# Window attention of a four-layer image model: scores as four 32-row products instead of one masked 128-row product

## The chip, the cores and the metric

The kernel is one program on one core of a Trainium2 chip. The metric is device time in microseconds (us) of one execution. Before the change three runs gave 7491.1, 7505.19 and 7510.78 us; the median is 7505.19 us. Most executions of one kernel agree within 0.3%.

## The reference: what is computed

The input is an fp32 image batch `x` of shape (4, 64, 128, 128). Eight stages follow each other (four pairs of a mixing layer and a feed-forward layer), each added to its input. The change touches only the first, a shifted-window attention:

```python
x = x + _L0_conv_ref(_ln_c(x), qkv_w, proj_w, proj_b, bias_table)
# DIM = 64, WS = 8 (windows of 8 x 8 = 64 pixels), NH = 4 heads,
# SHIFT = 4, HD = 16 channels of a head, SCALE = HD ** -0.5 = 0.25
#   q, k, v = the normalised image, rolled by 4, cut into windows, times qkv_w
#   scores  = SCALE * q @ k.T + relative position bias + shift mask
#   out     = softmax(scores) @ v, then proj_w and proj_b, rolled back
```

For each image, window and head the scores are a 64 x 64 matrix with a contraction over 16 channels. There are 256 windows in an image. The softmax is exact, with the row maximum taken off.

## The kernel before

Each stage is a function that writes one instruction stream for each engine (TensorE, VectorE, ScalarE, GpSimd and SyncE) by hand. Engines wait for each other only through semaphores, and each engine keeps the order in which its stream was written. `stage_window_attention` is the first stage; the others begin after it.

**Tiling.** Two images are worked on at once: 128 partitions are 2 images x 64 channels. `over_strips` runs twice (`bp`), each time over 16 strips of 8 image rows (16 windows side by side). The first strip and the last three are written out, the twelve between are a loop of four strips in a body. A strip has four steps, j = 0 to 3, of STEP = 4 windows for both images (T = 256 pixels). So the stage has 2 x 16 x 4 = 128 steps. `steps` gives each step s its neighbours: `after` is s + 1, `back1` is s - 1, `back2` is s - 2.

**One step, before the change.**

- TensorE, `qkv`: q and k of four windows into `pQK` (two products of 256 columns, line 567), v into `pV` (four of 128 columns, line 572).
- ScalarE, `save_qk`: `pQK` goes to SBUF in six copies. Two copies (line 455) write `qs`, one for each image g: the mask `gmask` keeps the 64 channels of image g, zeroes the others and holds SCALE. Four copies (line 458) write `ks`, one for each head: the mask `hmask` keeps the 16 channels of head k in both images and zeroes the rest.
- TensorE, `scores` (line 579): per window one product with 128 rows of contraction. Stationary are 128 columns (2 images x 64 queries), moving are 256 columns (4 heads x 64 keys). The output is `pS[128, STEP, NH, 64]`, two PSUM banks.
- VectorE, `softmax_shift`: bias added while `pS` is read (line 393; in step j = 3 the last window by itself at line 391), maximum (397), subtraction (399). ScalarE, `exponential` (464). VectorE, `softmax_sum`: sum (404), reciprocal (406). GpSimd, `normalise` (309).
- TensorE `turn_probs` (588), ScalarE `save_probs` (469), TensorE `values` (598: 16 products of 64 columns, each with 128 rows and 32 output partitions), ScalarE `save_values` (474), TensorE `project` (604), ScalarE `save_proj` (481).

**What goes between the steps.** The layer norm of the next strip is spread over the steps of the strip: `mean` (611), VectorE `center` (412), ScalarE `square` (487), `variance` (620), ScalarE `log` (492) and `root` (498), each with a change of activation table, and `write_h` on VectorE and GpSimd (225). At j = 2 GpSimd adds the residual of the strip before (321, 322), and TensorE turns the result (`turn_out`, 627) at the end of j = 2 and in j = 3; ScalarE saves it (503) and SyncE stores it.

**The order around the change.** On TensorE a step is `scores(s)`, `qkv(s+1)`, then the pieces of the norm, `values(s-2)`, `turn_probs(s-1)`, `project(s-2)`, more pieces of the norm, and `turn_out`. On ScalarE it is `save_qk(s+1)`, `save_values(s-2)`, a `square`, `exponential(s)`, `save_probs(s-1)`, `save_proj(s-2)`, and a `log`; at j = 2 `log` and `root` come before `save_qk`, and at j = 3 a `save_turned`. On VectorE it is `softmax_sum(s-1)`, at j = 1 the second `center`, `softmax_shift(s)`, at j = 2 `write_h`, `save_v(s+1)` (380), and at j = 0 the first `center`. The second `mean` of j = 0 waits for the first `center`, and the second `variance` of j = 1 waits for the first `log`; `scores` of the next step stands behind either. An fp32 product is two records of LDWEIGHTS and MATMUL in the trace.

Of the kernel before, what the change touches and what calls it, by code (L numbers as in the profile page):

```python
# [6 lines left out]
ALU = mybir.AluOpType  # L7
ACT = mybir.ActivationFunctionType
# [101 lines left out]
def stage_window_attention(nc, x, qkv_w, proj_w, proj_b, bias_table, tok):  # L110


    WS, NH, SHIFT = 8, 4, 4
    STEP = 4
    NSTEP = W // WS // STEP
    T = STEP * WS * WS
    STRIPS = H // WS
    NX = 4
    SCALE = float(C // NH) ** -0.5
    EPS = 1e-6  # L120
    with ExitStack() as ctx:
        a = Arena(nc, ctx, "wa")
# [10 lines left out]
        bits_qf = a.sb("bits_qf", [128, 4])  # L133
        bits_kf = a.sb("bits_kf", [128, 2, 64])
        gmask = a.sb("gmask", [128, 2])
        hmask = a.sb("hmask", [128, NH])
        half_mask = a.sb("half_mask", [128, 2, 16])
        table = a.sb("table", [128, 64, NH])
        bias = a.sb("bias", [128, 2, 2, NH, 64])
# [4 lines left out]
        h = a.sb("h", [128, 2, W // WS, 2, WS, WS])  # L144
        qs = a.sb("qs", [128, STEP, 2, 64])
        ks = a.sb("ks", [128, NH, T])
        vs = a.sb("vs", [128, NSTEP, STEP, 128])
# [9 lines left out]
        pQK = a.ps("pQK", [128, 2, T])  # L157
        pV = a.ps("pV", [128, STEP, 128])
        pS = a.ps("pS", [128, STEP, NH, 64])
        pT = a.ps("pT", [128, STEP, 2, 128])  # L160
# [128 lines left out]
        def _(pool):  # L289
            link = Link(pool, pool_done)  # L290

            for s, k in ((x1_turned, 1), (yr_ready, 1), (qkv_ready, 1), (scores_ready, 1), (v_saved, 1), (pt_saved, 1),
                         (proj_ready, 1), (scores_read, 1), (h_doubled, 1), (probs_turned, 2), (xt_saved, 2),
                         (pv_ready, NSTEP), (x1_ready, NX), (stored[0], 16), (stored[1], 16)):
                pool.sem_inc(s, k)
# [49 lines left out]
        def _(dve):  # L345
# [3 lines left out]

            for k, (bit, m) in enumerate([(5, 1), (2, 1), (4, 3), (6, 1)]):  # L350
                link(dve.tensor_scalar(bits_q[:, k:k + 1], iota_q[:, :], bit, m, SHR, AND))
                if k < 2:
                    link(dve.tensor_scalar(bits_k[:, k, :], iota_k[:, :], bit, m, SHR, AND))
            link(dve.tensor_copy(bits_qf[:, :], bits_q[:, :]))
            link(dve.tensor_copy(bits_kf[:, :, :], bits_k[:, :, :]))
            for g in range(2):
                link(dve.tensor_scalar(gmask[:, g:g + 1], bits_qf[:, 3:4], float(g), SCALE, ALU.is_equal, ALU.mult))
                link(dve.memset(half_mask[:, g, :], 0.0))
                link(dve.tensor_scalar(half_mask[:, g, :], half_mask[:, g, :], bits_qf[:, 3:4], float(g),
                                       ALU.add, ALU.is_equal))  # L360
            for k in range(NH):
                link(dve.tensor_scalar(hmask[:, k:k + 1], bits_qf[:, 2:3], float(k), None, ALU.is_equal))
# [21 lines left out]
            def softmax_shift(s, j, last):  # L384

                dve.wait_ge(scores_ready, s + 2)
                dve.wait_ge(probs_turned, s + 1)
                e, f = sc[:, j % 2, :, :, :], pS[:, :, :, :]
                n = STEP - 1 if j == NSTEP - 1 else STEP
                if n < STEP:  # L390
                    dve.tensor_tensor(e[:, n, :, :], f[:, n, :, :], bias[:, int(last), 1, :, :], ALU.add)
                r = bias[:, int(last), 0, :, :].rearrange("p h k -> p (h k)").unsqueeze(1).to_broadcast([128, n, NH * 64])
                dve.tensor_tensor(e[:, 0:n, :, :].rearrange("p w h k -> p w (h k)"),  # L393
                                  f[:, 0:n, :, :].rearrange("p w h k -> p w (h k)"), r,
                                  ALU.add).then_inc(scores_read, 1)
                dve.wait_ge(scores_read, s + 2)
                dve.tensor_reduce(mx[:, :, :], e, AX.X, ALU.max).then_inc(max_ready, 1)
                dve.wait_ge(max_ready, s + 1)
                dve.tensor_tensor(e, e, mx[:, :, :].unsqueeze(3).to_broadcast([128, STEP, NH, 64]),
                                  ALU.subtract).then_inc(shifted, 1)  # L400
# [46 lines left out]
        def _(act):  # L447
# [3 lines left out]
            def save_qk(s, j):  # L451
                act.wait_ge(qkv_ready, s + 2)
                act.wait_ge(scores_ready, s + 1)
                for g in range(2):
                    act.activation(qs[:, :, g, :], pQK[:, 0, :].rearrange("p (w q) -> p w q", q=64), ACT.Copy,  # L455
                                   scale=gmask[:, g:g + 1])
                for k in range(NH):
                    ins = act.activation(ks[:, k, :], pQK[:, 1, :], ACT.Copy, scale=hmask[:, k:k + 1])
                ins.then_inc(qk_saved, 1)
# [93 lines left out]
        def _(pe):  # L553
# [21 lines left out]
            def scores(s):  # L575
                pe.wait_ge(qk_saved, s + 1)
                pe.wait_ge(scores_read, s + 1)
                for w in range(STEP):
                    ins = pe.matmul(pS[:, w, :, :], qs[:, w, :, :].rearrange("p g q -> p (g q)"), ks[:, :, 64 * w:64 * w + 64],  # L579
                                    start=True, stop=True)  # L580
                ins.then_inc(scores_ready, 1)

# [2197 lines left out]
```

## Time and profile before

| | |
|---|---|
| Median of three runs | 7505.19 us |
| The profiled execution's own time | 7501.84 us, its span 7500.1 us |
| Busy over the span | PE 76%, PEld 51%, DVE 58%, ACT 50%, POOL 19% |
| Scores in the trace (line 579) | 42.7 to 1374.3 us, 1024 records |
| Busy from 42 to 1380 us | PE 1026.6, DVE 847.4, ACT 830.5, POOL 452.7 us |
| Granted clock there | 0.87 of full speed |

The engines are PE (TensorE's products), PEld (its weight loads, which overlap PE), DVE (VectorE), ACT (ScalarE), POOL (GpSimd) and SP (SyncE). The page's shares are means over eight stages; the scores are made only between 42 and 1380 us, which is 18% of the span. In a timeline a row is one group of neighbouring instructions of one line: its start, its length, engine, line and operation, output and inputs, shapes and count. Brackets hold the idle time of the engine before it and who ended that. Lengths of one record include its latency; how fast records follow each other is read from starts.

### The profile page before, as it was taken

How to read it: one execution, taken by the hardware profiler on the slowest of the kernel's cores; microseconds unless marked ns; L12 is line 12 of the kernel's file. 1: busy time of each engine (PE TensorE's matmuls, PEld its weight loads, DVE VectorE, ACT ScalarE, POOL GpSimd, SP SyncE). 2: the span in 40 equal slices, each digit the busy share in tenths (PEclk: the TensorE clock that was granted, in tenths of full speed). 3: DMA queues.
4: the chain of work that ended last, by engine and by line, in shares of the span. 5: the costliest groups of instructions: out<-in, count | busy, mean ns of one | idle time of the engine just before them, and what ended most of it. 6: DMA issues, size and time to landing. Idle time of an engine off the chain costs nothing. (4 is left out here: it accounts for less than half of the span.)

```text
span 7500.1 us, 128640 instructions
## 1 busy us (share of the span) xinstructions
PE 5733.5 (76%) x43616; PEld 3796.3 (51%) x43616; DVE 4316.2 (58%) x8974; ACT 3784.3 (50%) x7044; POOL 1430.9 (19%) x1334
## 2 busy tenths in 40 slices
PE   6776777666697777669979997541999999566666
PEld 4555556315354333359979994240555555332222
DVE  5665666563622777772223345538777777565565
ACT  5665666542643666462233323403666676454453
POOL 2332333432421000050000002312111121111110
PEclk9888888875698888869989998755999999777778
DMA  0101000121232767530000022214666676256666
GB/s 25 29 23 29 21 26 23 57 68 34 84 87 86 241 233 232 199 91 0 0 0 0 34 101 86 62 51 89 82 84 86 75 85 80 40 178 176 178 178 189
DMA packets 791912, 645.40 MB, mean 86 GB/s; under 512 B 494273, under 2 KB 641921, under 8 KB 791501
## 3 DMA queue, kind: packets, MB, share of 16 engines
q1 hardware_dynamic: 790477, 639.00, 35.0%
q8 instruction: 241, 3.95, 0.2%
q14 instruction: 170, 1.39, 0.1%
q0 software_dynamic: 1024, 1.05, 0.1%
HBM read 549.73 MB, written 90.20 MB: 85 GB/s over the span
## 5 line engine op out<-in xcount | busy, mean ns | idle before, releaser
L2300 PE MATMUL sw_pC<-sw_row,sw_wc 128*128 128x128 f32 x10160 | 1159.2, 274 | 56.8 <-DVE sw_row L2175 54.9
L2300 PEld LDWEIGHTS sw_pC<-sw_row,sw_wc 128*128 128x128 f32 x10160 | 1148.6, 191 | 58.1 <-DVE sw_row L2175 55.5
L2721 PE MATMUL sp_pC<-sp_work,sp_bands 64*64 64x512 f32 (+11 forms) x14592 | 986.1, 428 | 44.7 <-issue 44.7
L2721 PEld LDWEIGHTS sp_pC<-sp_work,sp_bands 64*64 64x64 f32 x14592 | 596.3, 133 | 437.8 <-issue 369.5
L2163 DVE SCALAR_TENSOR_TENSOR sw_row<-sw_pC,sw_y 128x128 f32<-128x128 f32 x1016 | 337.8, 332 | 792.7 <-PE sw_pC L2300 792.7
L2661 ACT ACTIVATE sp_pC<-sp_pC,sp_par 128x512 f32<-128x512 f32 x832 | 597.7, 740 | 375.5 <-PE sp_pC L2721 349.6
L1715 DVE TENSOR_TENSOR t_z<-t_z,t_ht 128x1024 f32<-128x1024 f32 x512 | 601.9, 1233 | 150.2 <-DMA t_z<-gate_rows 149.3
L1874 PE MATMUL t_pO<-t_z,t_ew 128*64 128x512 f32 x2048 | 557.5, 690 | 36.4 <-DVE t_z L1715 35.8
L2232 ACT ACTIVATE sw_y<-sw_row 128x128 f32 (+1 forms) x762 | 265.3, 348 | 593.6 <-DVE sw_row L2163 593.6
L2624 DVE TENSOR_TENSOR sp_work<-sp_work,sp_pC 128x512 f32<-128x512 f32 x512 | 351.0, 687 | 171.2 <-ACT sp_pC L2661 170.7
L1844 PE MATMUL t_pT<-t_ident,t_h 128*128 128x128 f32 x1024 | 195.8, 354 | 274.3 <-ACT t_gs L1771 157.9
L309 POOL TENSOR_TENSOR wa_sc<-wa_sc,wa_sm 128x1024 f32<-128x1024 f32 x128 | 243.3, 1901 | 712.0 <-DVE wa_sm L406 712.0
L1005 PE MATMUL c_pG<-c_ht,c_gate_cols 128*32 128x512 f32 x512 | 291.0, 703 | 80.7 <-ACT c_ht L950 80.7
L579 PE MATMUL wa_pS<-wa_ks,wa_qs 128*128 128x256 f32 x1024 | 322.2, 470 | 23.2 <-issue 18.3
L1874 PEld LDWEIGHTS t_pO<-t_z,t_ew 128*64 128x64 f32 x2048 | 153.0, 159 | 361.0 <-issue 263.1
L1844 PEld LDWEIGHTS t_pT<-t_ident,t_h 128*128 128x128 f32 x1024 | 156.2, 183 | 340.0 <-issue 275.8
L1780 ACT ACTIVATE t_oc<-t_pO 128x512 f32<-128x512 f32 x128 | 76.6, 599 | 497.4 <-PE t_pO L1874 497.4
L579 PEld LDWEIGHTS wa_pS<-wa_ks,wa_qs 128*128 128x128 f32 x1024 | 246.3, 244 | 110.1 <-issue 64.6
L2661 ACT ACTIVATE sp_side<-sp_pC,sp_par 64x512 f32<-64x512 f32 x384 | 297.0, 773 | 7.5
L2532 POOL COPY sp_bands<-sp_bands 128x1536 f32<-128x1536 f32 x96 | 141.4, 1473 | 815.0 <-PE sp_pC L2721 778.0
L393 DVE TENSOR_TENSOR wa_sc<-wa_pS,wa_bias 128x1024 f32<-128x1024 f32 (+1 forms) x128 | 147.8, 1155 | 252.9 <-PE wa_pS L579 250.2
L455 ACT ACTIVATE wa_qs<-wa_pQK,wa_gmask 128x256 f32<-128x256 f32 x256 | 107.3, 470 | 363.4 <-PE wa_pV L572 363.4
(346 smaller groups left out, 10834.3 us busy)
## 6 DMA issues: line engine op xcount, KB each, us to landing
t_z<-gate_rows SPq DMA_DIRECT2D x512, 512.0 KB, 6.7
sp_bands<-windows SPq DMA_DIRECT2D x128, 512.0 KB
c_xs<-tokens SPq DMA_DIRECT2D x128, 256.0 KB, 2.6
cb_xs<-tokens SPq DMA_DIRECT2D x128, 256.0 KB, 2.8
wa_xs<-in_x SPq DMA_DIRECT2D x64, 256.0 KB, 2.9
tokens<-wa_xt SPq DMA_DIRECT2D x128, 128.0 KB, 2.1
tokens<-cb_h SPq DMA_DIRECT2D x64, 256.0 KB, 2.4
t_xs<-tokens SPq DMA_DIRECT2D x32, 512.0 KB, 9.3
```

The source lines that it names most:

```text
L309: pool.tensor_tensor(p, p, r, ALU.mult).then_inc(probs_ready, 1)
L579: ins = pe.matmul(pS[:, w, :, :], qs[:, w, :, :].rearrange("p g q -> p (g q)"), ks[:, :, 64 * w:64 * w + 64], start=True, stop=True)
L1005: ins = pe.matmul(pG[m][E * b:E * b + E, :], gate_cols[:, m, :], ht[:, b % 2, :], start=True, stop=True)
L1715: dve.tensor_tensor(z[:, i, q, :], z[:, i, q, :], ht[:, m.k % HR, i, :], ALU.mult).then_inc(z_ready, 1)
L1844: ins = pe.transpose(pT[s][:, 128 * j:128 * j + 128], h[:, i, 4 * s + j, :, :].rearrange("p c d -> p (c d)"), ident[:, :])
L1874: ins = pe.matmul(pO[i][64 * s:64 * s + 64, :], ew[:, q, :], z[:, i, q, 512 * s:512 * s + 512], start=(q == 0), stop=(q == 3))
L2163: dve.scalar_tensor_tensor(row[par][c][:, :, PAD:PAD + P2], pC[c][:, 0:2 * P2].rearrange("p (b w) -> p b w", b=2), 0.0, line(sweep, c, i), ...
L2232: act.activation(line(sweep, c, i), row[par][c][:, :, PAD:PAD + P2], ACT.Copy).then_inc(saved[c], 1)
L2300: ins = pe.matmul(pC[c][:, 0:2 * P2], wc[:, sweep, m, :], row[1 - par][c][:, :, m:m + P2], start=(m == 0), stop=(m == 4))
L2624: return dve.tensor_tensor(new, old, rel, ALU.add)
L2661: return act.activation(out[rows_out, :], pC[q][rows_in, :], ACT.Relu, bias=par[rows_in, c, BI + i:BI + i + 1], scale=par[rows_in, c, SC + ...
L2721: ins = pe.matmul(out[halves[to], :, low * lo:low * hi], band[halves[k], (NV * g + j) % BANDS, q, AT[k][tap], :], v[halves[k], :, low * at ...
```

## The change

`qs` is saved once, with the constant SCALE, and `ks` twice, with a mask for even and one for odd heads: bit 4 of the partition, which picks 16 of each 32 partitions. `gmask` is gone. For each window, image g and pair of heads hp, one product contracts over the 32 partitions that hold these two heads' channels of this image. Stationary are the 64 queries and moving are 2 x 64 keys (even head, odd head); the output goes to the 64 partitions of image g, in PSUM bank hp. So `scores` has 16 products of 128 columns in a step in place of 4 of 256. Each of the four products of the last window raises `scores_ready`, and the waits count in fours. `softmax_shift` reads `pS` in the new order and writes `sc` in the old one, with as many elements and instructions as before.

```diff
-        gmask = a.sb("gmask", [128, 2])
-        hmask = a.sb("hmask", [128, NH])
+        hmask = a.sb("hmask", [128, 2])
-        qs = a.sb("qs", [128, STEP, 2, 64])
-        ks = a.sb("ks", [128, NH, T])
+        qs = a.sb("qs", [128, T])
+        ks = a.sb("ks", [128, 2, T])
-        pS = a.ps("pS", [128, STEP, NH, 64])
+        pS = a.ps("pS", [128, 2, STEP, 128])
...
-            for k, (bit, m) in enumerate([(5, 1), (2, 1), (4, 3), (6, 1)]):
+            for k, (bit, m) in enumerate([(5, 1), (2, 1), (4, 1), (6, 1)]):
...
-                link(dve.tensor_scalar(gmask[:, g:g + 1], bits_qf[:, 3:4], float(g), SCALE, ALU.is_equal, ALU.mult))
...
-            for k in range(NH):
+            for k in range(2):
                 link(dve.tensor_scalar(hmask[:, k:k + 1], bits_qf[:, 2:3], float(k), None, ALU.is_equal))
...
-                dve.wait_ge(scores_ready, s + 2)
+                dve.wait_ge(scores_ready, 4 * s + 8)
                 dve.wait_ge(probs_turned, s + 1)
-                e, f = sc[:, j % 2, :, :, :], pS[:, :, :, :]
+                e = sc[:, j % 2, :, :, :]
+                by_pair = e.rearrange("p w (a h) k -> p a w (h k)", a=2)
                 n = STEP - 1 if j == NSTEP - 1 else STEP
+                pairs = [bias[:, int(last), k, :, :].rearrange("p (a h) k -> p a (h k)", a=2) for k in range(2)]
                 if n < STEP:
-                    dve.tensor_tensor(e[:, n, :, :], f[:, n, :, :], bias[:, int(last), 1, :, :], ALU.add)
-                r = bias[:, int(last), 0, :, :].rearrange("p h k -> p (h k)").unsqueeze(1).to_broadcast([128, n, NH * 64])
-                dve.tensor_tensor(e[:, 0:n, :, :].rearrange("p w h k -> p w (h k)"),
-                                  f[:, 0:n, :, :].rearrange("p w h k -> p w (h k)"), r,
-                                  ALU.add).then_inc(scores_read, 1)
+                    dve.tensor_tensor(by_pair[:, :, n, :], pS[:, :, n, :], pairs[1], ALU.add)
+                dve.tensor_tensor(by_pair[:, :, 0:n, :], pS[:, :, 0:n, :],
+                                  pairs[0].unsqueeze(2).to_broadcast([128, 2, n, 128]), ALU.add).then_inc(scores_read, 1)
...
-                act.wait_ge(scores_ready, s + 1)
-                for g in range(2):
-                    act.activation(qs[:, :, g, :], pQK[:, 0, :].rearrange("p (w q) -> p w q", q=64), ACT.Copy,
-                                   scale=gmask[:, g:g + 1])
-                for k in range(NH):
+                act.wait_ge(scores_ready, 4 * s + 4)
+                act.activation(qs[:, :], pQK[:, 0, :], ACT.Copy, scale=SCALE)
+                for k in range(2):
                     ins = act.activation(ks[:, k, :], pQK[:, 1, :], ACT.Copy, scale=hmask[:, k:k + 1])
...
                 for w in range(STEP):
-                    ins = pe.matmul(pS[:, w, :, :], qs[:, w, :, :].rearrange("p g q -> p (g q)"), ks[:, :, 64 * w:64 * w + 64],
-                                    start=True, stop=True)
-                ins.then_inc(scores_ready, 1)
+                    cols = slice(64 * w, 64 * w + 64)
+                    for g in range(2):
+                        for hp in range(2):
+                            o = 64 * g + 32 * hp
+                            ins = pe.matmul(pS[64 * g:64 * g + 64, hp, w, :], qs[o:o + 32, cols], ks[o:o + 32, :, cols],
+                                            start=True, stop=True)
+                            if w == STEP - 1:
+                                ins.then_inc(scores_ready, 1)
```

## Rows read from the trace of the kernel before

**Rows 1.** The page's head: span and number of instructions.
```profile
span 7500.1 us, 128640 instructions
```
**Rows 2.** Tile view of wa_pS: lengths in ns (min/median/max), first and last start.
```profile
L579 PE MATMUL wa_pS<-wa_ks,wa_qs x1024: 379/379/796, 42.7 to 1374.3; 128*128 128x256 f32 x171
```
**Rows 3.** Waits, 42 to 1380 us: who waited for whom, us in total, times, longest.
```profile
DVE wa_sc L391 <- PE wa_pS L579: 83.8, 24, 5.0
```
**Rows 4.** Groups of ScalarE, 42 to 1380 us: busy us, mean ns of one.
```profile
L458 ACT ACTIVATE wa_ks<-wa_pQK,wa_hmask 128x256 f32<-128x256 f32 x510 | 200.0, 488 | 0.0
...
L474 ACT ACTIVATE wa_ov<-wa_pO 128x256 f32<-128x256 f32 x126 | 52.5, 417 | 4.8 <-PE wa_pO L598 4.8
```
**Rows 5.** Timeline of one step of the first half's last strip (no norm work).
```profile
664.85 1.89 PE L579 MATMUL wa_pS<-wa_ks,wa_qs 128*128 128x256 f32 x8
...
665.24 1.22 DVE L404 TENSOR_REDUCE wa_sm<-wa_sc 128x16 f32<-128x1024 f32 x1 [0.95 <-ACT wa_sc L464]
...
668.53 0.84 ACT L455 ACTIVATE wa_qs<-wa_pQK,wa_gmask 128x256 f32<-128x256 f32 x2 [2.05 <-PE wa_pV L572]
...
669.29 1.22 DVE L399 TENSOR_TENSOR wa_sc<-wa_sc,wa_mx 128x1024 f32<-128x1024 f32 x1
...
670.68 0.42 ACT L474 ACTIVATE wa_ov<-wa_pO 128x256 f32<-128x256 f32 x1
...
671.69 1.89 PE L579 MATMUL wa_pS<-wa_ks,wa_qs 128*128 128x256 f32 x8
...
672.08 1.22 DVE L404 TENSOR_REDUCE wa_sm<-wa_sc 128x16 f32<-128x1024 f32 x1 [0.96 <-ACT wa_sc L464]
```
**Rows 6.** Timeline of a whole strip, steps j = 0 to 3, 535 to 577 us.
```profile
541.58 0.67 DVE L412 TENSOR_TENSOR wa_xc<-wa_xs,wa_pL 128x512 f32<-128x512 f32 x1
...
542.61 1.22 DVE L404 TENSOR_REDUCE wa_sm<-wa_sc 128x16 f32<-128x1024 f32 x1 [0.36 <-ACT wa_sc L464]
...
545.20 1.23 DVE L393 TENSOR_TENSOR wa_sc<-wa_pS,wa_bias 128x1024 f32<-128x1024 f32 x1 [0.48 <-PE wa_pS L579]
...
549.89 1.10 ACT L464 ACTIVATE wa_sc<-wa_sc 128x1024 f32<-128x1024 f32 x1
...
556.08 2.84 PE L579 MATMUL wa_pS<-wa_ks,wa_qs 128*128 128x256 f32 x8
...
566.56 1.12 PE L627 MATMUL wa_pL<-wa_ident,wa_x 128*128 128x128 f32 x4 [2.52 <-POOL wa_x L322]
...
567.47 3.62 PE L579 MATMUL wa_pS<-wa_ks,wa_qs 128*128 128x256 f32 x8
...
571.13 0.42 DVE L391 TENSOR_TENSOR wa_sc<-wa_pS,wa_bias 128x256 f32<-128x256 f32 x1 [4.97 <-PE wa_pS L579]
...
573.23 0.84 ACT L455 ACTIVATE wa_qs<-wa_pQK,wa_gmask 128x256 f32<-128x256 f32 x2 [4.91 <-PE wa_pV L572]
...
576.77 1.22 DVE L404 TENSOR_REDUCE wa_sm<-wa_sc 128x16 f32<-128x1024 f32 x1 [1.24 <-ACT wa_sc L464]
```
**Rows 7.** Timeline of another strip: the scores of its steps j = 2 and j = 3.
```profile
1001.41 3.62 PE L579 MATMUL wa_pS<-wa_ks,wa_qs 128*128 128x256 f32 x8
...
1011.47 1.89 PE L579 MATMUL wa_pS<-wa_ks,wa_qs 128*128 128x256 f32 x8
```
**Rows 8.** Stretches: us, busy (x records) of PE, PEld, DVE, ACT, POOL, granted clock, DMA.
```profile
655.00:675.00 20.00, 17.20 (x187) 14.79 (x186) 16.02 (x18) 14.63 (x31) 5.14 (x3) 1.00 0.12 28
...
564.80:571.60 6.80, 5.04 (x14) 4.23 (x15) 1.80 (x4) 1.31 (x3) 3.56 (x3) 0.50 0.22 77
```
**Rows 9.** Timelines of TensorE: products on parts of the array, and their neighbours.
```profile
559.62 1.05 PE L572 MATMUL wa_pV<-wa_w_cols,wa_h 128*128 128x128 f32 x8
...
560.61 0.65 PE L598 MATMUL wa_pO<-wa_pt,wa_vs 128*32 128x64 f32 x32
...
561.20 1.09 PE L588 MATMUL wa_pT<-wa_ident,wa_sc 128*128 128x128 f32 x8
...
5320.69 2.64 PE L2721 MATMUL sp_pC<-sp_work,sp_bands 64*64 64x256 f32 x43
```

More of the change, by code:

```diff
@@ L290, in _ @@
             link = Link(pool, pool_done)
-            for s, k in ((x1_turned, 1), (yr_ready, 1), (qkv_ready, 1), (scores_ready, 1), (v_saved, 1), (pt_saved, 1),
+            for s, k in ((x1_turned, 1), (yr_ready, 1), (qkv_ready, 1), (scores_ready, 4), (v_saved, 1), (pt_saved, 1),
                          (proj_ready, 1), (scores_read, 1), (h_doubled, 1), (probs_turned, 2), (xt_saved, 2),
```

## Prediction

> **What bounds the kernel now.** I read the tile view of `wa_pS` first, then the waits of that stretch, then the timelines of one plain step and of one whole strip. The span is 7500.1 us [rows 1]. The scores lie between 42.7 and 1374.3 us [rows 2], so only some 1332 us and 128 steps (10.4 us each, 41.6 us a strip) are at stake. A sum of busy shares says nothing here, because no engine is full. What counts is a ring of waits.
>
> The plain step shows the ring [rows 5]. It lasts 671.69 - 664.85 = 6.84 us: scores start at 664.85, the first copy of `save_qk` at 668.53 (3.68 us later, with the scores and q, k, v of the next step on TensorE between them), `save_values` at 670.68 (2.15 us), the next scores at 671.69 (1.01 us, with the projection). Both things that the change cuts, the score products and the copies, lie on this ring. Beside it runs a second ring, VectorE and the exponential: from one sum to the next it takes the same 6.84 us (665.24 to 672.08) but holds 0.96 us of idle time, "ended by ACT" [rows 5]. The subtraction starts at 669.29 and lasts 1.22; the exponential (1.10 us) could then start at about 670.55 and end at 671.61, the sum at 671.65. So this ring by itself needs 671.65 - 665.24 = 6.41 us. That is what is late next.
>
> In a whole strip [rows 6] the scores start at 556.08 (j = 2) and 567.47 (j = 3), and sums at 542.61 (start of j = 1) and 576.77 (the end). From j = 2 to j = 3 pass 11.39 us, and the row before the scores of j = 3 (turn_out, 566.56) was released by GpSimd's residual. At j = 3 VectorE waits 4.97 us for the scores, which run at half clock: 3.62 us where the plain step has 1.89. The granted clock of that stretch is 0.50 [rows 8]. Such a wait at line 391 (a line that only j = 3 has) occurs 24 times, 83.8 us in all [rows 3], so in 24 of the 30 strips that are not a last one; in 6 it is missing.
>
> **The change part by part.**
>
> *Copies.* Six take 2.15 us from start to start [rows 5], or 0.36 each. Three go, 1.07 us. The remaining `qs` copy loses its per-partition scale and resembles line 474 (417 ns against 488 for line 458 [rows 4], and its successor may start earlier by about the same 0.1). I take 2.15 - 1.17 = 0.98 us; bounds 0.95 and 1.08.
>
> *Score products, full clock.* Before: 8 records, 1.89 us busy; the last one's own 379 ns [rows 2] off, and one distance of 0.215 added, TensorE is held 1.73 us. After: 32 records of 128 columns, each on 32 rows by 64 columns of the array. Such a shape isn't in the trace. The nearest is the last row of [rows 9]: 43 records of 256 columns on 64 x 64 pieces in 2.64 us, so 0.054 us apart (0.375 us off for the last), where a whole-array record of 256 columns takes 0.215. Four pieces work at once, two of them one above the other writing the same partitions in different banks, as here. For 128 columns that gives 0.027 each, 0.86 us for 32. The values row agrees for small pieces: 32 records of 64 columns in 0.65 us, 0.014 apart. The other bound is no overlap at all: 32 x 0.107 = 3.4 us. I take 0.86, by the nearer row. *Change of array shape:* from v (559.62, last record 0.78 later) to values (560.61) pass 0.21 where 0.11 is usual; back, the transposes start 0.59 after the values do, whose 32 records need about 0.45 (0.65 less 0.2 for the end of the last) [rows 9]. I take 0.10 on entry and 0.15 on leaving. So the scores hold TensorE 1.11 instead of 1.73 us, and VectorE may read 0.7 us earlier (the last record is about 0.11 shorter too). At half clock all of it doubles but the fixed part: 3.45 to 2.0, and 1.5 us earlier to VectorE.
>
> *A rule against it.* The rows just used show records of small pieces 0.02 us apart. The Trainium skill (TensorEngine Tiling (Array Packing), Instruction Overhead) says that each product has about 60 cycles of overhead. If that came on top, 32 records would add an estimated 0.8 us and TensorE would gain nothing; the values row speaks against it, and this is rival A below.
>
> *VectorE.* The bias addition reads as many elements in as many instructions, only in another order; I take 0 (bounds -0.1 and +0.3 us a step; its neighbours with broken-up patterns go at the same rate). The set-up drops four tiny operations before the first strip: 0, hidden by the loads. The waits count to four times the number, no wait is added.
>
> *Now where it lies, strip by strip.* I go by the start of the sums.
> - j = 0: the sum at 542.61 waited 0.36 us for the exponential, which stood behind ScalarE's copies. With ScalarE ahead, it starts when `center` ends (541.58 + 0.67 = 542.25, [rows 6]): 0.33 us gained. VectorE is now the bound.
> - j = 1: the exponential starts at 549.89, 7.28 us after the sum. New: the second mean still waits for `center`, 0.96 us later come the scores, 1.2 us later VectorE reads, with addition, maximum and subtraction at 1.25 each (1.22 and a short gap) about 6.0. On ScalarE: scores 1.11, q, k, v 1.75 and latency, copies 0.98 at 5.0, then `save_values` and a square, 6.3. So 6.3 against 7.28: 0.98 gained, and the logarithm, the variance and the scores of j = 2 follow at once.
> - j = 2: scores, copies and additions come earlier, but the path is variance, log, root, GpSimd's half of `write_h`, residual, turn_out. It issues nothing that the change cuts. Gained: 0. This cover hides about 2.5 us of saved work. In another strip the same stretch took 10.06 us [rows 7] rather than 11.39: there the late scores kept VectorE's subtraction and GpSimd apart. With early scores I expect the longer pattern everywhere: the 6 strips without the wait lose about 1.0 us.
> - j = 3: scores 1.5 earlier; q and k then still run at half clock, so `save_qk` starts only 0.6 us earlier (573.23 to 572.6); copies 1.17 less. Both rings end 1.7 us earlier at 575.1 instead of 576.77. The average wait is 83.8 / 24 = 3.5 us, not 4.97, so part of these strips catch the higher clock halfway; I take 1.55 on average.
>
> *Sum.* 24 strips x (0.33 + 0.98 + 1.55) = 68.6. Six strips x (0.33 + 0.98 - 1.0) = 1.9. Two last strips with three plain steps x 0.43 = 2.6. Two first steps, where copies (1.17) and half-clock scores (1.5) stand bare, 5.3. Together 78.4 us. The profiled execution took 7501.84 us and becomes 7423; the median of the runs shown lies 3.4 us higher, so I predict 7427 us.
>
> **The rivals.**
>
> *A: TensorE gains nothing* (overhead or only two pieces at once), only the copies count. By the same walk j = 0 gains 0.33, j = 1 about 0.6, j = 3 about 0.66: 24 x 1.6 + 6 x 0.2 + 5 = 44 us, 7461. Chance 0.13.
>
> *B: the pieces don't overlap.* Scores hold 3.7 us. j = 0 costs +0.6, j = 1 +1.3, j = 3 +2.3, j = 2 nothing: 31 x 4.2 = 130 us slower, 7635. It decides from about 0.08 us a record. Against it stand both piece rows. Chance 0.05.
>
> *C: the clock.* TensorE holds full clock now in j = 0 and 1 and in plain steps with 17.20 of 20 us busy, and fell to half in the stretch of j = 3 [rows 8] after it had waited for GpSimd. With shorter scores it rests more, about 1.0 to 1.5 us in 6.6. If it fell at j = 0 and 1 too, the ring of j = 0 would take about 10 us instead of 6.6 and j = 1 some 2.5 more: 31 x 5.9 - 78 = 105 us slower, 7610. It decides when a step's rest is enough for the fall; strips lose their gain when one in three steps does. For it: 24 strips fell after a rest of 2.5 us. Against it: plain steps rest 1 us and hold. Chance 0.06.
>
> *D: the walk is right, but VectorE takes it back:* the addition in its new order or collisions with GpSimd cost 0.7 us a step. In j = 0, where VectorE is the bound, and in j = 1 that undoes most: gain 15, 7490. Chance 0.09. More instructions at the loop's jumps (four of them) could cost 3 us each, 14 us; that is in the range.
>
> **How the numbers follow.** The forecast has 0.67. Measurements of this kernel tell 0.3%, 22 us, from no change. Faster by more: forecast, A, and a little of D: 0.80. Within: most of D and weak forms of A and C: 0.09. Slower: B and C: 0.11. The range takes in A (7461) with some of its weaker form, 7470, and downwards the case that strips keep the short pattern of j = 2 (6 strips or more, up to 1.0 each), the full 1.73 at j = 3 and a clock that rises earlier: about 110 us, 7395.
>
> **What the profile will show.** Right: scores 32 records of about 1.1 us at full clock; from the first copy to `save_values` 1.0 us where values are done; VectorE's waits at 391 down to about 2 us each; j = 2 to j = 3 still 11.4 us; plain steps 6.4 us with VectorE never idle but for the exponential. Wrong: scores over 1.7 us (A, B), a granted clock of 0.5 in the steps j = 0 and 1 (C), line 393 over 1.3 us (D). A gain at j = 2 would mean that I misread its path.

## The result and the profile after

The changed kernel takes 7379.18 us (median of 4 runs, 7364.29 to 7382.94) against 7504.66 us for the kernel before, measured beside it: a ratio of 0.9833, 95% interval 0.9818 to 0.9847. The gain is 125 us where 78 were forecast, and the time lies below the range. The profiled execution took 7380.56 us, 121.3 less than that of before.

First the page: span, instructions, and TensorE's granted clock in 40 slices.

```profile
span 7378.8 us, 134524 instructions
...
PEclk8887888865898888689989998656999999787778
```

There are 5,884 more instructions than in [rows 1], and the span is 121.3 us shorter. The rest is read as before. The tile view of the scores:

```profile
L579 PE MATMUL wa_pS<-wa_ks,wa_qs x4096: 267/318/472, 41.5 to 1271.2; 32*64 32x128 f32 x196
its engine sat idle before it (us, times) until:
  issue: 12.4, 4
```

The waits from 35 to 1280 us (total, times, longest):

```profile
DVE wa_sc L391 <- PE wa_pS L579: 95.9, 28, 3.7
```

ScalarE's groups in the same time (busy us, mean ns, idle before):

```profile
L454 ACT ACTIVATE wa_ks<-wa_pQK,wa_hmask 128x256 f32<-128x256 f32 x256 | 106.8, 473 | 0.0
...
L452 ACT ACTIVATE wa_qs<-wa_pQK 128x256 f32<-128x256 f32 x128 | 49.2, 384 | 315.1 <-PE wa_pV L568 315.1
```

The scores lie in a stretch of 1229.7 us instead of 1331.6 [rows 2]. The wait at line 391 is 3.4 us on average, in 28 strips; before it was 3.5 us in 24 [rows 3]. The masked copies take about what they took (473 ns against 488 [rows 4]), the `qs` copy with a constant scale 384 ns.

The timeline of the strip that answers to [rows 6], from the sum that opens j = 1 on (start, us, engine, line, shapes, idle time before and its releaser):

```profile
502.41 1.22 DVE L402 TENSOR_REDUCE wa_sm<-wa_sc 128x16 f32<-128x1024 f32 x1
...
506.76 0.39 ACT L452 ACTIVATE wa_qs<-wa_pQK 128x256 f32<-128x256 f32 x1 [2.59 <-PE wa_pV L568]
507.04 0.83 ACT L454 ACTIVATE wa_ks<-wa_pQK,wa_hmask 128x256 f32<-128x256 f32 x2
...
508.95 1.05 ACT L460 ACTIVATE wa_sc<-wa_sc 128x1024 f32<-128x1024 f32 x1
...
515.40 1.99 PE L579 MATMUL wa_pS<-wa_ks,wa_qs 32*64 32x128 f32 x32
...
518.64 4.53 POOL L224 TENSOR_TENSOR wa_h<-wa_xc,wa_sq 128x960 f32<-128x960 f32 x3 [5.12 <-ACT wa_sq L494]
...
520.04 1.89 DVE L397 TENSOR_TENSOR wa_sc<-wa_sc,wa_mx 128x1024 f32<-128x1024 f32 x1
...
523.13 2.34 POOL L320 TENSOR_TENSOR wa_x<-wa_xs,wa_yr 128x992 f32<-128x992 f32 x1
...
525.73 1.12 PE L628 MATMUL wa_pL<-wa_ident,wa_x 128*128 128x128 f32 x4 [3.53 <-POOL wa_x L321]
...
526.78 1.98 PE L579 MATMUL wa_pS<-wa_ks,wa_qs 32*64 32x128 f32 x32
...
528.90 0.42 DVE L391 TENSOR_TENSOR wa_sc<-wa_pS,wa_bias 128x256 f32<-128x256 f32 x1 [3.58 <-PE wa_pS L579]
...
533.83 1.22 DVE L402 TENSOR_REDUCE wa_sm<-wa_sc 128x16 f32<-128x1024 f32 x1 [0.52 <-ACT wa_sc L460]
```

From sum to sum the strip takes 533.83 - 502.41 = 31.42 us where [rows 6] gives 34.16: 2.74 gained, and the walk had 0.98 + 0 + 1.7 = 2.68 for these three steps. The exponential of j = 1 starts 6.54 us after the sum (7.28 before, 6.3 forecast). Between the scores of j = 2 and j = 3 pass 11.38 us, as before. The scores at half clock take 1.98 us (3.62 before).

Of the plain steps (no norm work), two scores in a row (6.13 us apart; 6.84 before), the copies, and two sums in a row:

```profile
615.79 1.10 PE L579 MATMUL wa_pS<-wa_ks,wa_qs 32*64 32x128 f32 x32
...
616.92 1.22 DVE L402 TENSOR_REDUCE wa_sm<-wa_sc 128x16 f32<-128x1024 f32 x1 [0.52 <-ACT wa_sc L460]
...
618.96 0.38 ACT L452 ACTIVATE wa_qs<-wa_pQK 128x256 f32<-128x256 f32 x1 [0.79 <-PE wa_pV L568]
...
620.01 0.39 ACT L470 ACTIVATE wa_ov<-wa_pO 128x256 f32<-128x256 f32 x1
...
621.92 1.10 PE L579 MATMUL wa_pS<-wa_ks,wa_qs 32*64 32x128 f32 x32
...
623.21 1.22 DVE L402 TENSOR_REDUCE wa_sm<-wa_sc 128x16 f32<-128x1024 f32 x1 [0.52 <-ACT wa_sc L460]
```

The scores take 1.10 us (1.89 before), the copies 620.01 - 618.96 = 1.05 from start to start (2.15 before, 0.98 forecast). From sum to sum pass 623.21 - 616.92 = 6.29 us (6.84 before, 6.41 forecast).

**Where the 121.3 us of span went.** I cut the stage at the scores that open each strip (their j = 0) and compared strip with strip:

| Part | Gained, us | Forecast, us |
|---|---|---|
| 20 ordinary strips | 52.5 (2.62 each) | 47.0 (2.35 each) |
| 8 strips at the loop's four jumps | 36.3 (4.54 each) | 18.8 |
| the two first strips | 7.9 | 10.0 |
| two last strips, start and end of the stage | 5.5 | 2.6 |
| a later stage of unchanged code (the first with `t_` names) | 17.1 | 0 |
| the other stages | 2.0 | 0 |

(Forecast: the mean of the 24 and the 6 strips is 70.5 / 30 = 2.35.) The ordinary strips came out near the walk. Two things did not: the jumps, and a stage that the change doesn't touch. Both show as idle time "ended by issue", that is, with nothing in the trace that it waited for. Ahead of the scores TensorE had eight such stops in the kernel before, two a jump; its tile view of the scores says (us, times):

```profile
  issue: 18.3, 8
```

After the change it has four, 12.4 us (the tile view above). And ScalarE's waits in that later stage, of the kernel before, 2395.9 to 3149.5 us (total, times, longest):

```profile
ACT t_mom L1745 <- DVE t_mom L1672: 35.5, 1, 35.5
ACT t_h L1753 <- issue: 16.3, 3, 6.1
```

In the kernel after, the same view of 2292.2 to 3028.8 us has the first and lacks the second; what line 1754 still waits is a real wait of 0.8 us:

```profile
ACT t_mom L1746 <- DVE t_mom L1673: 34.4, 1, 34.4
...
ACT t_h L1754 <- DVE t_nm L1680: 0.8, 3, 0.5
```

### The profile page after: what moved, and what is told of

It reads as the page before. It is cut to its first block and busy times, and to the rows that moved or that the text cites. A ratio compares the mean times of both kernels' runs of the same rounds, so it can differ in the third digit from the quotient of the medians.

```text
span 7378.8 us, 134524 instructions
## 1 busy us (share of the span) xinstructions
PE 5643.9 (76%) x46688; PEld 3706.0 (50%) x46688; DVE 4306.4 (58%) x8970; ACT 3650.0 (49%) x6660; POOL 1439.8 (20%) x1334
## 3 DMA queue, kind: packets, MB, share of 16 engines
q0 software_dynamic: 1024, 1.05, 0.1%
## 5 line engine op out<-in xcount | busy, mean ns | idle before, releaser
L1644 POOL TENSOR_TENSOR passes<-passes,t_xs 128x512 f32 (+1 forms) x64 | 105.2, 1644 | 832.5 <-DMA t_xs<-tokens 832.5
L392 DVE TENSOR_TENSOR wa_sc<-wa_pS,wa_bias 128x1024 f32<-128x1024 f32 (+1 forms) x128 | 147.8, 1155 | 201.5 <-PE wa_pS L579 201.5
L2735 PE MATMUL sp_pC<-passes,sp_roll 128*128 128x512 f32 x128 | 59.8, 622 | 246.2 <-DVE passes L2603 246.2
```

The source lines that it names most:

```text
L1644: pool.tensor_tensor(x_of(m, i), x_of(m, i), xs[:, :, :], ALU.add).then_inc(joined, 1)
```

## The experiments

"The stage" is the first one, with the `wa_` names: 1401.2 us before, 1299.0 after. "The later stage" is the first with the `t_` names: 753.7 before, 736.6 after. Stage times come from one profiled execution each. Ratios are against the kernel before.

### Are the stops due to where the code lies?

**pad_pe**: the changed kernel with 64 semaphore increments at the head of TensorE's stream. They touch nothing but the position of all that follows.

```diff
+        pad = a.sem("pad")
...
+            for _ in range(64):
+                pe.sem_inc(pad, 1)
```

> The kernel after with 64 semaphore increments at the head of TensorE's stream (a semaphore that nobody reads), so that every later TensorE instruction lies 64 instructions further on; the work is the same. In the trace of before TensorE stopped twice at each jump back of the strip loop (before the scores and again after 4 of 8 records, 3.1 and 2.1 us in the shown one), in the trace of after once. Theory S (the second stop depends on where the loop's first instruction lies in the instruction supply): the second stop comes back four times, 7388 to 7396 against 7379. Rival U (the second stop belonged to the long records of the old scores): 7379 within 5, one stop a jump.

Measured: 7391.49 us, 0.9847 (0.983 to 0.9863), 12 us slower than the change. Its tile view of the scores:

```profile
  issue: 22.6, 8
```

The second stop per jump is back, and the stage takes 1312.8 us, 13.8 more: 3.4 for each of the four jumps. The eight strips at the jumps alone take 333.2 us instead of 315.1, which is 18.1 more; the other strips came out some 4 us shorter this time. The later stage keeps its gain (735.4). In the changed kernel, then, all or nearly all of the 15.3 us that the jumps gained beyond ordinary strips hangs on the position of TensorE's code.

**pad_act**: the same with 96 increments at the head of ScalarE's stream.

```diff
+        pad = a.sem("pad")
...
+            for _ in range(96):
+                act.sem_inc(pad, 1)
```

> The kernel after with 96 semaphore increments at the head of ScalarE's stream, as many as the copies that the change took out of its text, so that all later ScalarE code lies where it lay before. Between the two traces the first top-2 feed-forward stage, whose code is the same, became 17 us shorter (753.7 to 736.6 us), because three stops of 5 to 6 us of ScalarE before t_h, ended by nothing that the profile shows, are missing. Theory S: they come back, 7390 to 7400, that stage 750 to 755 us. Rival V (they come and go from one execution to the next): 7379 within 6, and that stage 737 to 754 at random.

Measured: 7396.11 us, 0.9848 (0.9831 to 0.9864), 17 us slower. The stage hardly moves (1302.8). The later one takes 758.5 instead of 736.6, and the row that the change had removed is back; ScalarE's waits of pad_act, 2296.1 to 3054 us:

```profile
ACT t_h L1757 <- issue: 16.9, 3, 5.8
```

All fourteen traces of this document say the same. Where ScalarE has as many instructions ahead of that stage as in the kernel before (before, act_six, swap_before, swap_six and pad_act), the row is there, with three stops and 13.8 to 16.9 us; in the other nine it is missing. So the stops don't come and go from one execution to the next. The branch records tell where they are: right behind the three jumps of that stage's loop. In the kernel before, ScalarE's next instruction follows the branch after 5.5, 6.8 and 6.1 us; in the changed kernel it follows after 0.2 to 0.3 us.

**pad_before**: the kernel before with 192 increments ahead of TensorE's stream and 160 ahead of ScalarE's.

```diff
+        pad = a.sem("pad")
...
+            for _ in range(160):
+                act.sem_inc(pad, 1)
...
+            for _ in range(192):
+                pe.sem_inc(pad, 1)
```

> The kernel before with nothing but semaphore increments that nobody reads at the heads of two streams: 192 on TensorE, 160 on ScalarE, so that the loop's first TensorE instruction and all later ScalarE code lie at the same place in blocks of 256 instructions as in the kernel after. Theory S (what stops is the instruction supply, by the place of the code): the second stop at the four jumps goes (-14 us), the first top-2 stage falls from 754 to 737 us: 7470 to 7480 with no work saved. Rival T (the place counts in no such blocks, or only together with the new code): 7495 to 7515.

Measured: 7499.97 us (10 runs), 0.9998 (0.9989 to 1.0007). The total missed the 7470 to 7480 that I expected, because two parts cancel: the stage became 17.6 us longer (1418.8 against 1401.2), the later stage 18.4 shorter. The later stage fell from 753.7 to 735.3, the 18.4 us that I wanted, without a change to the attention. TensorE's stops fell from 8 to 4, but the scores began late. Its tile view of them:

```profile
L584 PE MATMUL wa_pS<-wa_ks,wa_qs x1024: 379/379/767, 56.3 to 1391.8; 128*128 128x256 f32 x171
...
  issue: 13.2, 4
```

They start 13.6 us after those of [rows 2]; 64 or 96 increments had delayed nothing (41.4 and 41.8 us in pad_pe and pad_act), so which of the two paddings did it is open. And the eight strips at the jumps took 350.2 us instead of 351.4: in the old kernel, as far as this run tells, the second stop is worth next to nothing, though in the trace of before it lasts 1.2 to 2.1 us each time. In the changed kernel it lasts 2.1 to 2.9 us (pad_pe) and costs 3.4 us a jump or more. I had taken it for additive; it is not. So the 13.8 us are what the position is worth in the changed kernel; had it been set right in the old kernel first, next to nothing would have been gained there.

The lengths say something of the rule. On ScalarE the change took 96 instructions away, pad_before added 160, and both removed the stops, while pad_act, at the old position, kept them. Positions counted modulo 256 (or 64 or 128) would do that; one pair of lengths doesn't show it.

### Which half brings the gain?

**act_six**: the change with three copies more, into a buffer that nobody reads. It keeps the products, and undoes what ScalarE saves.

```diff
+        kx = a.sb("kx", [128, 3, T])
...
+                for k in range(3):
+                    act.activation(kx[:, k, :], pQK[:, 1, :], ACT.Copy, scale=hmask[:, k % 2:k % 2 + 1])
```

> The kernel after with three more copies of k into a buffer that nobody reads, so ScalarE again makes six copies in a step while TensorE keeps the 32-row products: the products' part of the gain alone. Theory R (both cuts lie on the ring scores, q/k/v, copies, save_values, projection): the copies take 2.1 instead of 1.0 us from start to start, and of the 3.4 us that a strip gained between the two traces about half goes again: 7430 to 7445 us against 7379. Rival P (the products alone made the gain, the copies were hidden): 7380 to 7390. Rival Q (the copies alone made it): 7490 to 7505.

Measured: 7462.96 us, 0.9939 (0.9922 to 0.9955), a gain of 44 us on 7507.31, the median of before beside it (the same for pad_pe, pad_act and the next run). Beside the change it is 84 us slower, where I expected 51 to 66. The stage takes 1368.1, 33.1 less than before, the later one 753.2: ScalarE has its old number of instructions, and its stops.

**full_three**: the kernel before with three of its six copies; it leaves out the queries of image 1 and the keys of heads 2 and 3, whose scores become zero.

```diff
+            link(pool.memset(qs[:, :, :, :], 0.0))
+            link(pool.memset(ks[:, :, :], 0.0))
...
-                for g in range(2):
+                for g in range(1):
...
-                for k in range(NH):
+                for k in range(2):
```

> The kernel before with three of the six copies left out (one of q, two of k): the other parts of the two buffers are zeroed once, so image 1's queries and heads 2 and 3 get zero scores; the 128-row products, their number and everything else stay. The copies' part of the gain alone. Theory R: 45 to 65 us faster than before, 7440 to 7460. Rival P: 7495 to 7505. Rival Q: 7380 to 7400.

Measured: 7407.74 us, 0.987 (0.9854 to 0.9887): 100 us, where I expected 45 to 65 and rival A had 44. But not all of it is the copies' own: ScalarE has lost its stops here too, and the later stage takes 738.3 us, 15.4 less. The stage takes 1320.3, which is 80.9 less. In the stage the two halves would add up to 33.1 + 80.9 = 114 us, and the change brings 102.2.

Part of why the copies bring so much shows in j = 2 of an ordinary strip, in the timeline of full_three:

```profile
562.87 3.54 PE L581 MATMUL wa_pS<-wa_ks,wa_qs 128*128 128x256 f32 x8
...
566.21 2.63 POOL L225 TENSOR_TENSOR wa_h<-wa_xc,wa_sq 128x960 f32<-128x960 f32 x3 [4.17 <-ACT wa_sq L500]
...
568.96 3.20 DVE L401 TENSOR_TENSOR wa_sc<-wa_sc,wa_mx 128x1024 f32<-128x1024 f32 x1
...
572.90 3.33 PE L581 MATMUL wa_pS<-wa_ks,wa_qs 128*128 128x256 f32 x8
```

Here the scores come so late that VectorE's subtraction begins after GpSimd's `write_h`, which then takes 2.63 us. In the changed kernel it begins in the middle of it, and `write_h` takes 4.53. The single records show how: `write_h` on GpSimd is one long piece and two short ones, and the two engines take turns. The subtraction, begun beside the long piece, ends 1.08 us after it; the first short piece (0.25 us alone) then ends 0.11 us after the subtraction, and the second 0.11 us after the first piece of VectorE's own half of `write_h`. From j = 2 to j = 3 pass 10.03 us here and 11.38 there. This is the pattern of [rows 7]. Of the 28 strips that are neither first nor last, 6 have a step j = 2 under 10.5 us before, 21 in this experiment, and none after the change. The forecast had seen that the change gives this pattern up, for 6 strips; it had not seen that the copies alone would bring it to most. On average j = 2 takes 11.03 us before and 10.33 here, over 28 strips 20 of the 37 us by which the stage's gain exceeds 44. The rest has no experiment of its own. Ordinary strips take 41.09 us before (median), 38.02 here, 37.69 after. With the copies gone, the products add only 21.3 us in the stage. 11.4 of these lie at the eight strips of the jumps, where full_three still has two stops each time and the change one.

**same_piece**: the change with the loops over g and hp outside, w inside: four products in a row on the same part of the array.

```diff
-                for w in range(STEP):
-                    cols = slice(64 * w, 64 * w + 64)
-                    for g in range(2):
-                        for hp in range(2):
-                            o = 64 * g + 32 * hp
+                for g in range(2):
+                    for hp in range(2):
+                        o = 64 * g + 32 * hp
+                        for w in range(STEP):
+                            cols = slice(64 * w, 64 * w + 64)
```

> The kernel after with the loops of the scores turned over: the four windows of one image and pair of heads follow each other, so that neighbouring products use the same 32 x 64 piece of the array. Theory N (four pieces work at once only if neighbouring products differ in piece, since they start in order): the scores of a step take about 3.4 us at full clock in place of 1.1, and the kernel loses 60 to 130 us, 7440 to 7510. Rival O (the order doesn't matter): 1.1 us and 7379.

Measured: 7467.48 us, 0.9949 (0.9929 to 0.9969), 88 us slower than the change. The scores at full clock, in its timeline:

```profile
545.05 2.56 PE L579 MATMUL wa_pS<-wa_ks,wa_qs 32*64 32x128 f32 x32
```

2.56 us instead of 1.10, less than the 3.4 of no overlap at all. In its single records, those on the same part start 0.107 to 0.109 us apart, and only near a change of part do two parts run at once. So the order of the loops carries the overlap. The Trainium skill (TensorE: Matmul & The Clock Gate, Part 3: Packing small matmuls — row/col tiling) states that products start and end in program order. That four in a row on one part queue agrees with it; what happens at the change of part doesn't. The first record of the second part starts at 545.55 us, ahead of the last three of the first part (545.65, 545.76 and 545.87, the last of them the one that raises `scores_ready`). This head start is why the step takes 2.56 us and not 3.4.

### VectorE as the next bound

**no_max**: the change without the maximum (zero is subtracted), so that VectorE has 1.22 us less in every step.

```diff
+            link(dve.memset(mx[:, :, :], 0.0))
...
-                dve.tensor_reduce(mx[:, :, :], e, AX.X, ALU.max).then_inc(max_ready, 1)
+                dve.sem_inc(max_ready, 1)
```

> The kernel after without the maximum of the softmax (a zero is subtracted instead; the reduction of 1.22 us is left out in each step). Theory D (in j = 0 and in the plain steps the ring of VectorE and the exponential is the bound now): plain steps fall from 6.14 to about 5.3 us, where the TensorE and ScalarE ring takes over, j = 0 and 1 lose 0.5 to 1 us each, 7325 to 7350. Rival E (TensorE and ScalarE are still the bound everywhere): 7370 to 7380.

Measured: 7357.38 us (2 runs), 0.9803 (0.9783 to 0.9822), 22 us faster than the change, which is no more than the noise; the stage, 1274.6 us, is 24.4 shorter. That lies between the two expectations. j = 0 falls from 8.00 to 6.95 us (medians), j = 1 from 11.81 to 11.54, j = 2 stays at 11.4, and j = 3 grows from 6.83 to 7.38. The second plain step falls from 6.14 to 5.51 (5.3 expected). VectorE bounds j = 0 and the plain steps, as the forecast said, but each gives back less than the 1.22 us that went. Elsewhere the gain is small or negative; what the strip hangs on there this run doesn't separate.

### The path through j = 2

The forecast put 0 on j = 2, since GpSimd's `write_h`, residual and turn_out bound it. To test it, an exchange: at j = 2 GpSimd does the residual first, which has its inputs early.

```diff
+                    if j == 2 and not first:
+                        residual(n - 1, (k - 1) % NX)
...
-                    if j == 2 and not first:
-                        residual(n - 1, (k - 1) % NX)
```

**swap_before** has it in the kernel before, **swap_after** in the changed one.

> The kernel before, with GpSimd's two pieces at j = 2 exchanged: residual of the last strip first, then its half of write_h. The residual needs only save_proj of j = 1 and then no longer waits for the root. Theory W (the path from j = 2 to j = 3 is variance, log, root, write_h on GpSimd, residual, turn_out): the scores of j = 3 come 2.5 to 3 us earlier in each of 30 strips, 70 to 90 us faster than before, 7415 to 7435. Rival X (what sets j = 3 is TensorE and the copies, or write_h is then late for the q, k, v of the next strip): under 20 us, 7487 to 7510.

> The same exchange in the kernel after. Theory W: the saved work of j = 2, which the path through GpSimd hid, counts now too, and the stretch from j = 2 to j = 3 is no longer 11.4 us but 8 to 8.5: 85 to 110 us faster than after, 7270 to 7295, so the exchange is worth more here than in the kernel before. Rival X: 7360 to 7385.

Measured: 7390.56 us, 0.9847 (0.983 to 0.9863), and 7269.27 us, 0.9681 (0.9665 to 0.9698). The exchange brings some 115 us before, where I expected 70 to 90, and 110 after. The expectation that it would be worth more in the changed kernel missed (in the stage 109.0 us against 107.8). The timeline of swap_after at j = 2:

```profile
470.53 2.28 POOL L320 TENSOR_TENSOR wa_x<-wa_xs,wa_yr 128x992 f32<-128x992 f32 x1
...
472.45 1.98 PE L579 MATMUL wa_pS<-wa_ks,wa_qs 32*64 32x128 f32 x32
...
475.69 4.53 POOL L224 TENSOR_TENSOR wa_h<-wa_xc,wa_sq 128x960 f32<-128x960 f32 x3 [2.68 <-ACT wa_sq L494]
...
479.60 1.10 PE L579 MATMUL wa_pS<-wa_ks,wa_qs 32*64 32x128 f32 x32
```

The residual runs in the time in which GpSimd had waited for the root. `write_h` still takes 4.53 us, but the scores of j = 3 no longer stand behind it: 7.15 us after those of j = 2 instead of 11.38, and at full clock. This shows what bound j = 2.

**swap_three** is full_three with the exchange, **swap_six** is act_six with it: they ask what each half is worth once j = 2 no longer hides it.

> The kernel full_three (old products, three of six copies left out, so image 1's queries and heads 2 and 3 get zero scores) with GpSimd's two pieces at j = 2 exchanged. Without the exchange the new products were worth 21 us of the first stage once the copies were gone (1320.3 to 1299.0), 14 of them a stop of the instruction supply, because j = 2 rose from 10.05 to 11.45 us. Theory G (early scores push VectorE's subtraction into GpSimd's write_h and so delay the residual and turn_out): with the residual out of the way the products are worth 30 to 50 us beyond swap_after, 7300 to 7320. Rival H (the products are worth nothing beside the copies for another reason): within 20 us of swap_after, 7270 to 7290.

> The kernel act_six (new products, three copies more into a buffer that nobody reads) with the same exchange: the products' part alone without the collision. Theory G: 55 to 75 us faster than swap_before, 7315 to 7335. Rival H: the products bring no more than the 44 us of act_six, 7345 to 7360.

Measured: 7300.79 us, 0.973 (0.9715 to 0.9745), and 7317.52 us, 0.9748 (0.9733 to 0.9763). Both lie in the ranges of theory G. Beyond the copies the products are worth 7300.79 - 7269.27 = 31.5 us (28.5 without the exchange), beyond the products the copies 48.3 (83.8 without; some 16 us of either are the later stage's stops). The products gain little more than without the exchange (in the stage 28.3 us against 21.3), the copies less; that the collision had hidden much of the products' worth is thus not borne out. Where the copies go shows in the steps j = 3 (medians over the strips that are neither first nor last): with and without the three extra copies 8.24 and 6.83 us, but 6.33 in both once the exchange lets j = 3 run at full clock. At full clock VectorE's ring bounds the step, and ScalarE's copies fit beside it. For the change as a whole this evens out: 7390.56 - 7269.27 = 121 us with the exchange, 125 without. The 2.5 us that the forecast saw hidden at j = 2 of each strip were no reserve that the exchange frees.

**swap_log**: swap_after with the first logarithm of the norm moved ahead on ScalarE, right behind the exponential of j = 1, before `save_probs` and `save_proj`.

```diff
+                    if j == 1 and not last:
+                        log(n + 1, 0)
...
-                    if j == 1 and not last:
-                        log(n + 1, 0)
```

> A further step on swap_after: at j = 1 ScalarE's first logarithm comes right behind the exponential instead of behind save_probs and save_proj (1.5 us of work), and with it the variance and the scores of j = 2. Theory W (in j = 1 the path is exponential, save_probs, save_proj, table, log, variance, scores): 1.3 to 1.5 us a strip, 30 to 45 us faster than swap_after, 7225 to 7240. Rival Y (turn_probs, values and projection of j = 2 then wait for the late save_probs and give it back, or VectorE is the bound): 7260 to 7275.

Measured: 7212.58 us (5 runs, 7199.71 to 7217.55), 0.961 (0.9597 to 0.9623). That is 57 us faster than swap_after, more than expected, and 167 us faster than the changed kernel. j = 1 falls from 11.81 to 9.77 us, an ordinary strip from 34.09 to 32.06, and 28 x 2.03 = 57. The wait at line 391, 95.9 us after the change, had gone with the exchange already and stays away. Who waited for the scores, in their tile view of swap_log:

```profile
  DVE wa_sc L391: 0.4, 2
```

## Why the prediction was wrong, point by point

**The failed step: code length was priced as a possible loss only.** The last sentence on the rivals gave "more instructions at the loop's jumps" up to 14 us of loss (four times 3 us are 12), in the range, and nothing to any other stage. The sum itself had no term for it. TensorE's stream grew, ScalarE's shrank, and both new positions held fewer stops: one stop a jump instead of two (13.8 us in the changed kernel, by pad_pe), three stops less in the later stage (17 to 22 us, by pad_act and the stage's time). Together 31 to 36 of the 43 us by which the profiled execution missed its 78. The rows were in the trace of before: 18.3 us at 8 places ahead of the scores, 16.3 us at 3 places in the later stage. I read only the stretch of the change. The size was partly luck: the paddings show the same work at other code positions with 12 and 17 us less gain, and both positions fell well here.

**The strips: near.** 20 ordinary ones gained 2.62 us each; the forecast's mean was 2.35. The difference is 7.6 us over 28 strips. In the strip shown, j = 1 gained 0.79 from sum to sum (forecast 0.98), j = 2 -0.16 (0), j = 3 2.11 (1.7). j = 0, whose opening sums are 535.70 before and 496.09 after, gained 542.61 - 535.70 - 6.32 = 0.59 (0.33).

**The scores: right.** 32 records in 1.10 us at full clock and 1.98 at half (1.11 and 2.0). The overlap of pieces was read from another stage's 64 x 64 records, and it held for 32 x 64. The rule of about 60 cycles a product, weighed ahead of the result (TensorEngine Tiling (Array Packing), Instruction Overhead, in the Trainium skill), would have added an estimated 0.8 us for 32 records; no such time is in the 1.10.

**The copies: right in size, wrong in worth.** 1.05 us a step instead of 0.98. But rival A gave the copies alone 44 us, and full_three gained 80.9 in the stage. I had walked A through one strip with the long pattern of j = 2, and the copies by themselves move most strips to the short one (about 20 us).

**VectorE: right as the bound, wrong in the wait.** The plain step was to be 6.41 us from sum to sum and is 6.29. With less to wait for, VectorE has only the exponential's 0.52 us idle between two sums. The L391 wait should fall to about 2 us and stayed at 3.4: VectorE is ready earlier too, so the wait doesn't measure the gain.

**The rivals.** A fell with the 1.10 us. B (no overlap) fell with it too. same_piece goes part of the way to it: scores of 2.56 us, against 1.11 in the forecast and 3.7 in B. On the straight line between the two times, 208 us apart, that would be some 117 us; it cost 88. C (the clock): over 35 to 1280 us the granted clock is 0.86, as good as before, and it is 1.00 both from 503 to 511 us (j = 1 of the strip shown) and from 615 to 624 us (plain steps). D: the bias addition takes 1155 ns on average with its short forms, 1.22 to 1.23 for a full one, as before.

**Median and profiled execution** differ by 1.4 us here and by 3.4 in the forecast: nothing.

**What stays open.** Why the second stop at a jump costs 3.4 us in the changed kernel and nearly nothing in the one before isn't shown. Nor is it shown which code positions give a stop, or what the engine waits for in one: each padding tried one length. The ordinary strips' surplus of 5.5 us and the 5.5 us at the ends of the stage (2.6 forecast) have no experiment of their own.

## What to carry to other kernels

A change that alters the number of instructions on an engine moves all code behind it. List the idle times "ended by issue" in all stages, not only in the changed one, and give their sum a place on both sides of the range: here some 31 us hung on it, and paddings of 64 and 96 idle instructions gave 12 and 17 of them back. When work is cut at one step of a strip, ask where the same cut shifts two engines against each other at the next; and before cutting work, look for an operation that stands in line though its inputs have long been ready: two such moves were worth 167 us here, more than the change.

## What the runs showed of the hardware

- Stops with no cause in the trace depend on code position: 2.3 to 3.3 us each on average on TensorE at a loop's jump (before, after, pad_pe, pad_before), up to 6.1 on ScalarE at the jumps of the later stage's loop. 96 increments ahead of ScalarE's stream made a stage 22 us longer; 160 (with 192 on TensorE) made it 18 us shorter in the other kernel. 192 increments ahead of TensorE's stream and 160 ahead of ScalarE's delayed the first scores by 13.6 us.
- Products on parts of the array overlap with products on another part that come close behind in the order of issue: 16 products of 128 columns (32 records) in 1.10 us when the part changes with every product, in 2.56 when it changes with every fourth. At such a change the next part started ahead of the last three records of the one before.
- GpSimd's operations on two SBUF operands and VectorE's subtraction or `write_h`, also on two, take turns. `write_h` took 2.63 us without the subtraction beside it and 4.53 with it, and the subtraction 1.23 alone, 1.89 beside `write_h` and 3.20 beside the residual. In the changed kernel all 32 subtractions that began beside a GpSimd operation ended 1.08 to 1.09 us after that operation's end.
- A ScalarE copy of 128 x 256 with a constant scale takes 384 ns, with a scale per partition 473.
